# A hand-ordered decoder layer: first turn, factor additions and fifth turn rewritten

## What is computed

```python
# 1: gated recurrent attention; q = quantise a row to 8 bits, t = round a weight to -1, 0, 1
i, f, g = q(rms(x)) @ t(Wi), sigmoid(q(rms(x)) @ t(Wf)), q(rms(x)) @ t(Wg)
h[c] = f[c] * h[c - 1] + silu(i)[c] * (1 - f[c])          # scan over tokens
x = layernorm(x + q(rms(rms(g) * gw * silu(h))) @ t(Wo))
# 2: four experts, chosen by the token's id; one matrix per expert, used three times
x = layernorm(x + (silu(x @ C[e].T) * (x @ C[e].T)) @ C[e].T)
# 3: eight 512 x 512 factors
x = layernorm(x + sum_r(x @ F[r]) / sqrt(8) + bias)
```

## Time and profile before

| | us |
|---|---|
| median of 3 runs | 372.42 |
| lowest, highest | 371.88, 375.5 |
| the profiled execution, whole | 369.25 |
| its span | 367.5 |
| PE, DVE, ACT, POOL busy | 285.9, 225.3, 230.8, 200.5 |

### The profile page before, as it was taken

One profiled execution on the slowest core, in us unless ns is written; L12 is line 12 of the kernel. 1 busy time (PEld: TensorE's weight loads), 2 busy tenths in 40 slices (PEclk: granted clock), 3 DMA queues, 4 the chain that ended last, 5 costly groups with the idle time before them and its releaser, 6 DMA issues.

```text
span 367.5 us, 5728 instructions
## 1 busy us (share of the span) xinstructions
PE 285.9 (78%) x1506; PEld 215.5 (59%) x1518; DVE 225.3 (61%) x488; ACT 230.8 (63%) x456; POOL 200.5 (55%) x381
## 2 busy tenths in 40 slices
PE   1376467575687997998998895999399999999960
PEld 1254235242575675676876674777288888888640
DVE  4799999999387579839656753452234444444420
ACT  4779877977367696777777666256145555555441
POOL 2455867858546348466565837546044444444542
PEclk9998859695599999999999999899799999999996
DMA  8999968753883530003012101201401111100000
GB/s 261 389 387 374 228 117 160 143 138 89 198 162 62 94 115 2 29 40 105 0 48 75 54 29 77 69 29 42 131 29 57 52 38 59 57 30 24 28 7 0
DMA packets 17406, 37.02 MB, mean 101 GB/s; under 512 B 1503, under 2 KB 1631, under 8 KB 17376
## 3 DMA queue, kind: packets, MB, share of 16 engines
q0 software_dynamic: 6496, 15.74, 18.6%
q1 hardware_dynamic: 10880, 20.92, 17.2%
HBM read 26.68 MB, written 10.76 MB: 102 GB/s over the span
## 4 chain that ended last, share of the span: by engine, by line
PE 36%; POOL 6%; issue 6%; DMA 5%; ACT 4%; DVE 3%; POOLq 0%; ACTq 0%; DVEq 0%; SPq 0%
PE bank_m L1264 4%; PE bank_m L1268 4%; PE bank_m L1265 4%; PE bank_z L1264 3%; PE bank_z L1265 3%; DMA sorted_rows<-r,place 3%; PE bank_z L1268 3%; PE bank_y L1264 3%; PE bank_y L1265 3%; PE bank_y L1268 3%; DMA rows<-sorted_rows 2%; POOL n_d L313 2%; PE bank_tr L1235 2%; PE bank_q L1235 2%; POOL x L353 1%
## 5 line engine op out<-in xcount | busy, mean ns | idle before, releaser
L312 POOL TENSOR_SCALAR n_v<-n_dev 128x1 f32<-128x1 f32 (+1 forms) x46 | 10.1, 220 | 60.9 <-ACT x L626 28.5
L1264 PE MATMUL bank_y<-c_hi,h_hi 128*128 x76 | 32.2, 424 | 3.1 <-ACT h_hi L594 1.5
L1264 PE MATMUL bank_z<-c_hi,a_hi 128*128 x76 | 32.8, 432 | 1.9 <-ACT a_hi L594 1.9
L1264 PE MATMUL bank_m<-f_hi,m_hi 128*128 128x512 f32 x76 | 31.6, 416 | 3.4 <-DVE f_lo L876 2.6
L895 DVE TENSOR_TENSOR act_z<-bank_z,act_z 128x512 f32<-128x512 f32 x19 | 13.1, 691 | 34.3 <-ACT act_z L608 34.3
L358 POOL DMA_INDIRECT out<-r,token_of x19 | 20.6, 1087 | 23.1 <-ACT r L633 19.9
L1265 PE MATMUL bank_z<-c_lo,a_hi 128*128 x76 | 31.7, 417 | 0.0
L1265 PE MATMUL bank_y<-c_lo,h_hi 128*128 x76 | 30.8, 405 | 0.0
L313 POOL TENSOR_TENSOR n_d<-n_v,minus_half 128x1 f32<-128x1 f32 (+1 forms) x46 | 28.3, 615 | 3.8
L1265 PE MATMUL bank_m<-f_lo,m_hi 128*128 128x512 f32 x76 | 30.1, 396 | 0.0
L353 POOL TENSOR_TENSOR x<-x,bias_b 128x512 f32<-128x512 f32 x19 | 25.0, 1315 | 9.0 <-PE bank_q L1235 8.8
(11 more groups left out here) (205 smaller groups left out, 855.6 us busy)
## 6 DMA issues: line engine op xcount, KB each, us to landing
f_sum<-in_factors POOLq DMA_DIRECT2D x7, 1024.0 KB, 10.6
rows<-sorted_rows SPq DMA_DIRECT2D x19, 256.5 KB, 2.9
xs<-in_x SPq DMA_DIRECT2D x8, 512.0 KB, 6.2
c_stage<-in_ctx_t SPq DMA_DIRECT2D x4, 1024.0 KB, 14.3
sorted_rows<-pad_row SPq DMA_DIRECT2D x1, 1539.0 KB, 20.6
w_stage<-in_wf_t SPq DMA_DIRECT2D x1, 1024.0 KB, 8.4
w_stage<-in_wi_t SPq DMA_DIRECT2D x1, 1024.0 KB, 10.6
w_stage<-in_wg_t SPq DMA_DIRECT2D x1, 1024.0 KB, 12.8
```

The source lines that it names most:

```text
L1264: t.matmul(bank[:], hi[:, c, :], w_hi(c), start=(c == 0), stop=False)
```

## The change

**First turn.** SP loads factor 0 ahead of ctx(1) and x(3). POOL does `number_slots` before `weight_ready(W_F)`. DVE does `quantise_x(1)` and `order_slots` before the first weight's scale, and `rescale_f(0, 1)` only behind the rounding of W_G. PE makes the total of W_G inside `project_f(0)`, between its two halves, and ACT does `tanh_f(0, 1)` behind `weight_ready(W_G)`.

**Factor additions.** They stand at other places in POOL's list: 2 before turn 1, 3 in turn 1 behind `scale_g(1)`, 4 in turn 2 behind `power_1(0)` and ahead of `scale_o(1)`, 5 at the end of turn 2, 6 in turn 4 behind `token_of_row(1)`, 7 in turn 4 behind `scatter_rows(3)`. `high_of_factors` moves, in turn 5, from behind `silu_z(2)` to behind `forget(5, 1)`, ahead of `high_a(3)`.

**Turn 4.** It is written out apart from the loop, with another order on all engines. The loop begins with turn 5 and is otherwise the same, with the conditions on n gone.

```diff
 SP
+                sp.dma_start(f_sum[:], chunked(factors[0:D, :])).then_inc(s.factor0, 16)
                 load_ctx(1)
                 load_x(3)
-                sp.dma_start(f_sum[:], chunked(factors[0:D, :])).then_inc(s.factor0, 16)
 POOL
+                number_slots()
                 weight_ready(W_F)
-                number_slots()
...
                 power_x(2)
+                add_factor(2)
...
                         scale_g(g)
-                        add_factor(2)
+                        add_factor(3)
                         power_x(g + 2)
                     elif turn == 2:
-                        add_factor(3)
                         power_1(p - 1)
+                        add_factor(4)
                         scale_o(p)
                         pool.wait_ge(s.padded, 16)
                         scatter_rows(p - 1)
-                        add_factor(4)
                         scale_g(g)
                         power_x(g + 2)
+                        add_factor(5)
                     else:
...
-                        add_factor(5)
...
                 scatter_rows(MERGE - 1)
                 token_of_row(0)
+                g, p, n = MERGE + 1, MERGE, 1
+                scale_o(p)
+                quantise_o(p)
+                token_of_row(n)
                 add_factor(6)
+                power_2(n - 1)
+                scale_g(g)
+                number_rows(p)
+                token_of_row(n + 1)
+                power_1(p)
+                add_bias(n - 1)
+                power_2(n)
+                scatter_rows(p)
+                add_factor(7)
+                power_x(g + 2)
 ACT
                 tanh_f(0, 0)
-                tanh_f(0, 1)
                 weight_sum(W_O)
                 weight_ready(W_G)
+                tanh_f(0, 1)
...
+                square_1(p - 1)
+                high_a(n - 1)
+                square_o(p, 0)
+                norm_1(p - 1)
+                square_o(p, 1)
+                silu_z(n - 1)
+                high_h(n - 1)
...
+                square_g(g, 1)
+                high_a(n)
+                x_by_channel(g + 1)
+                max_row(g + 1)
+                square_2(n - 1)
+                silu_h(g, 0)
+                norm_2(n - 1)
+                silu_h(g, 1)
+                silu_z(n)
+                o_by_channel(p)
...
-                    if turn == MERGE + 2:
-                        high_of_factors()
...
                         forget(g, 1)
+                    if turn == MERGE + 2:
+                        high_of_factors()
                     high_a(n)
 DVE
+                quantise_x(1)
+                order_slots()
                 weight_scale(W_F)
                 round_weights(W_F)
-                order_slots()
                 weight_scale(W_I)
                 round_weights(W_I)
                 rescale_f(0, 0)
-                quantise_x(1)
-                rescale_f(0, 1)
                 weight_scale(W_G)
                 round_weights(W_G)
+                rescale_f(0, 1)
...
+                output(p, 0)
+                output(p, 1)
+                low_a(n - 1)
+                max_o(p, 0)
+                max_o(p, 1)
+                hidden(n - 1)
...
 PE
                     by_channel(g, W_F, 0, bank_c, s.zf)
+                    if g == 0:
+                        weight_total(W_G)
...
+                silu_h_by_token(p)
+                transpose_a(n - 1)
+                up(n - 1)
+                project_f(g)
+                transpose_h(n - 1)
+                project_i(g)
+                pe.wait_ge(s.o, GT * MERGE)
+                down(n - 1)
+                project_g(g)
+                transpose_a(n)
+                pe.wait_ge(s.oqt, p)
+                transpose_x(g + 1)
+                spread_max(g + 1)
+                up(n)
+                pe.wait_ge(s.xqt, g + 2)
+                transpose_o(p)
+                transpose_h(n)
+                project_back(p)
+                transpose_a(n + 1)
+                down(n)
+                pe.wait_ge(s.oqt, p + 1)
+                transpose_m(n - 1)
+                up(n + 1)
```

More of the change, by code:

```diff
@@ L448, in _ @@
                 token_of_row(0)
+                g, p, n = MERGE + 1, MERGE, 1
+                scale_o(p)
+                quantise_o(p)
+                token_of_row(n)
                 add_factor(6)
-                for turn in range(MERGE + 1, N_GROUPS + 1):
+                power_2(n - 1)
[8 more added lines that the diff above has]
+                power_x(g + 2)
+                for turn in range(MERGE + 2, N_GROUPS + 1):
                     g, p, n = turn, turn - 1, 2 * turn - LEAD
@@ L455, in _ @@
                     power_2(n - 1)
-                    if turn == MERGE + 1:
-                        add_factor(7)
                     token_of_row(n)
@@ L460, in _ @@
                         scale_g(g)
[L461 to L465, removed]
+                    add_bias(n - 2)
+                    power_3(n - 3)
+                    store(n - 3)
                     number_rows(p)
-                    if n >= 2:
-                        power_3(n - 2)
+                    power_3(n - 2)
                     token_of_row(n + 1)
                     power_1(p)
-                    if n >= 2:
-                        store(n - 2)
+                    store(n - 2)
                     add_bias(n - 1)
@@ L693, in _ @@
                         high_of_ctx(turn + 1, range(KC))
[L695 to L699, removed]
+                g, p, n = MERGE + 1, MERGE, 1
+                square_1(p - 1)
[5 more added lines that the diff above has]
+                high_h(n - 1)
+                tanh_f(g, 0)
+                tanh_f(g, 1)
+                silu_i(g, 0)
+                silu_i(g, 1)
+                forget(g, 0)
+                forget(g, 1)
+                square_g(g, 0)
+                square_g(g, 1)
[8 more added lines that the diff above has]
+                o_by_channel(p)
+                square_x(g + 2, 0)
+                high_h(n)
+                square_x(g + 2, 1)
+                high_a(n + 1)
+                square_1(p)
+                high_m(n - 1)
+                square_2(n)
+                norm_1(p)
+                norm_2(n)
+                for turn in range(MERGE + 2, N_GROUPS + 1):
                     g, p, n = turn, turn - 1, 2 * turn - LEAD
                     silu_z(n - 1)
-                    if turn == MERGE + 2:
-                        high_of_factors()
                     square_o(p, 0)
@@ L724, in _ @@
                         silu_h(g, 0)
-                    if n >= 2:
-                        high_m(n - 2)
+                    high_m(n - 2)
                     if is_group(g):
                         silu_h(g, 1)
-                    if n >= 3:
-                        square_3(n - 3)
+                    square_3(n - 3)
                     silu_z(n)
@@ L734, in _ @@
                         square_x(g + 2, 0)
-                    if n >= 3:
-                        norm_3(n - 3)
+                    norm_3(n - 3)
                     high_h(n)
-                    if n >= 2:
-                        square_3(n - 2)
+                    square_3(n - 2)
                     if is_group(g + 2):
@@ L743, in _ @@
                     square_1(p)
-                    if n >= 2:
-                        norm_3(n - 2)
+                    norm_3(n - 2)
                     high_m(n - 1)
@@ L1048, in _ @@
                     residual_1(p)
-                low_a(0)
-                for turn in range(MERGE + 1, N_GROUPS + 1):
+                g, p, n = MERGE + 1, MERGE, 1
+                output(p, 0)
[4 more added lines that the diff above has]
+                hidden(n - 1)
+                rescale_f(g, 0)
+                rescale_f(g, 1)
+                low_h(n - 1)
+                rescale_i(g, 0)
+                rescale_i(g, 1)
+                scale_x(g + 1)
+                quantise_x(g + 1)
+                gate_i(g, 0)
+                scans(g, 0)
+                gate_i(g, 1)
+                scans(g, 1)
+                residual_2(n - 1)
+                low_a(n)
+                weigh_g(g, 0)
+                weigh_g(g, 1)
+                hidden(n)
+                max_x(g + 2, 0)
+                max_x(g + 2, 1)
+                low_h(n)
+                residual_1(p)
+                low_a(n + 1)
+                residual_2(n)
+                low_m(n - 1)
+                for turn in range(MERGE + 2, N_GROUPS + 1):
                     g, p, n = turn, turn - 1, 2 * turn - LEAD
@@ L1077, in _ @@
                         scans(g, 1)
[L1078 to L1081, removed]
+                    residual_3(n - 3)
+                    low_m(n - 2)
                     if is_group(g):
@@ L1088, in _ @@
                         max_x(g + 2, 1)
-                    if n >= 2:
-                        residual_3(n - 2)
+                    residual_3(n - 2)
                     low_h(n)
@@ L1301, in _ @@
```

(16 more changed lines are left out.)

## The result

The changed kernel takes 379.78 us (median of 4 runs, 376.84 to 382.05) beside 373.57 us (median of 4 runs, 371.88 to 375.5) for the one before: ratio 1.0172, 95% interval 1.0124 to 1.0221. It is slower by 6.4 us, as forecast in size. Its profiled execution took 379.08 us, with a span of 377.3 against 367.5, so between the two profiles lie 9.8 us and not 6.4. Single executions of one kernel spread widely, those of the kernel before from 369.3 to 378.8 over the study, and its profile is the lowest of them: 369.25, where no other execution was under 369.4. The two profiles show where the loss arises; its size is taken from the ratios. The ratios leave out executions over 1.5% above the fastest of the same kernel in their job, among them three at 440.9, 716.2 and 717.3 us that nothing here explains.

The account below looks back on a forecast made before the run. It took DMA to bound up to about 50 us, DVE turns 1 to 3, PE from turn 4. Front 0, mix 5.4 and clock 1.0 gave +6.4 us on the 372.4 median: 378.8, range 372.5 to 382.5.

Parts of the forecast that it names:

- front 0: First turn and additions 2 to 5: no net effect by the end of turn 2, bounds 1.3 us gained and 3 lost.
- mix 5.4: Turn 5: the first mix starts at 148.2 instead of 142.76, 5.4 us later, and the end moves with it.
- clock 1.0: PE at the first mix: idle stretches drop its clock to half, costing 1.0 us, at most 2.5.
- Addition 7 and the first mix: Turns 4 and 5: addition 7 lands 13.5 us behind the scatter, and the mix starts 6.4 us after that.
- Turn 4: Early silu transposes and later addition 6 bring silu_z(1), and the scatter with it, 2.3 us earlier; between 1.8 and 3.2.
- rival (b): Turns 1 and 2: addition 1 lands at 46.8 as before, scale_o(0) and DVE are 3 us late, total 381.8; chance 0.13.
- The first turn's 1.3 us: First turn: DVE work moved into its idle time ahead of the first weight's scale gains about 1.3 us by turn 1.

Follow-up runs that it names:

- front_back: The changed kernel with additions 2 to 5 at their places in the kernel before: ratio to before 0.9969.
- seven_early: The changed kernel with addition 7 moved from behind scatter_rows(3) to ahead of power_1(3) in turn 4: 373.98 us, ratio to before 1.0046.
- both_back: The changed kernel with additions 2 to 5 as before and addition 7 ahead of power_1(3): ratios to before 0.9839 and 0.9897 in two jobs.
- f_lo_first_2: both_back with DVE's low_of_factors ahead of low_a(3) in turn 5, second job: ratio to before 0.9858.
- six_back: both_back with addition 6 back ahead of scale_o(3), its place before: ratio to before 0.9933.
- silu_behind_up: both_back with PE's silu transposes back behind up(0) in turn 4, and the DVE and ACT work with them: ratio to before 1.0003.
- first_turn_only: The kernel before with only the first turn's new order: ratio to before 1.0005.
- four_behind: seven_early with addition 4 behind scatter_rows(0) instead of ahead of scale_o(1): ratio to before 0.9975.
- seven_late_in_before: The kernel before with addition 7 behind scatter_rows(3) and high_of_factors behind forget(5, 1): ratio to before 1.0141.

## Why the prediction was right, and where its terms were not

**The forecast of 378.8 us is met by 379.78, but not by its terms.** It summed front 0, mix 5.4, clock 1.0. The late mix is as forecast; the front is not, and the number came out right in part by luck.

**Addition 7 and the first mix: right.** From the scatter to the first mix it had 13.5 + 6.4 = 19.9 us, measured 18.1 in two kernels and 18.3 in a third (front_back). The term that is too large is the landing: f_hi starts 12.2 us behind the scatter (145.91 - 133.70), since the addition took 11.2 us and not 12.4. The rest was 151.76 - 145.91 = 5.9 for 6.4. Slot 3's load took 6.6 us for 7.1. The late mix costs 18.1 - 11.6 = 6.5 us by the pair after and seven_early.

**Turn 4: right.** It had 2.3 us, with 1.8 "if up(0) gains no clock and 3.2 if it gains all". In after the clock did not rise (0.79 us for up(0)'s first product, as in the earlier trace rows) and the stretch is 38.3 - 36.5 = 1.8 us shorter. In both_back and f_lo_first_2 that product took 0.49 us, the full clock, and the stretch was 2.6 and 2.4 us shorter than in before. That ACT's queue takes back part of PE's gain is seen too: up(1) gains 2.2 us (19.5 for 21.7), silu_z(1) 24.1 for 25.4, which is 1.3. What the forecast treated as a sum, silu first and addition 6 later, is not one: each alone gives nothing (six_back and silu_behind_up). Against first_turn_only, where the old turn 4 took 39.9 us, the gain would be larger, so its size is known to a microsecond or so.

**The front: wrong.** "I take 0 for the front part, with bounds of 1.3 gained and 3 lost" is the step that failed. Measured by seven_early against the two both_back profiles it is 4.5 to 6.0 us lost. The mechanism was there, in the text and in rival (b), but two terms of its sum were too small. Addition 2 was given 9.0 us and up to one of contention; it took 11.8 in after, 14.3 in seven_early and 15.1 in four_behind, issued at 41.5 to 44.1 while the padding of `sorted_rows` and the load of group 4 were under way, so addition 3 landed at 66.6 and not at 61.4 to 63.4. That these two transfers made it slow was not tested. And scale_o was given 2.7 us; it took 49.93 - 45.02 = 4.9 in turn 1 and 71.38 - 67.71 = 3.7 in turn 2. The stalls came at 71.4 instead of 65.4 to 67.4. Rival (b) had named another cause, addition 1 landing at 46.8; it landed at 43.5, near the 42.8 forecast. Its effect came about all the same: DVE's quantise_o(0) is 49.96 - 47.63 = 2.3 us late in turn 1. The first turn's 1.3 us were not seen in any time.

The Trainium skill's rule of the shared ports ("SBUF — State Buffer", SBUF: two separate sides) was weighed there, and the forecast took the undisturbed 2.7 us because scale_o(0) would stand behind DVE's rounding of W_O. It did not: its first operation took 1.71 us beside DVE's second rounding, which started at 44.68. That agrees with the rule, but it does not carry the whole 4.9. In seven_early the second rounding ended at 42.68, ahead of scale_o(0), which still took 3.7 us; and in its turn 2 DVE was idle for all of scale_o(1), which took 3.1 us, its first operation 0.70 instead of 0.19. In all six places where scale_o stands right behind an addition this operation took 0.70 to 1.71 us, elsewhere up to the first mix 0.19 or 0.20, and it begins before the row of the addition's own issue (1.3 to 2.2 us) has ended. So standing behind an addition has a price of its own, which the forecast put at nothing.

**The clock: right in after, and not certain elsewhere.** PE waited 5.15 and 2.41 us ahead of the mix, the first product took 0.79 us, and the first eight cost 1.4 us more than in before. In seven_late_in_before PE had waited 5.68 and 1.46 us, and the mix ran at full clock. The forecast's bound of 2.5 us for twelve products is 2.1 by its own rows: (99.73 + 1.58 - 96.15) - (115.94 + 1.09 - 114.00).

**How it came out right in sum.** By stations, after should be 4.9 - 1.8 + 5.9 + 0.8 = 9.8 us above the profile of before, which is what the two profiles show and 3.4 more than the forecast's sum. The front's missing 4.9 us is only partly made up by a late mix that was taken too large (5.4 for 5.9 - 1.8 = 4.1). The ratio says 6.4, with 4.6 to 8.3 in its interval. The difference is the choice of profiles: that of before is 4.3 us under the median of its runs, that of after 0.7 under its own. With the front's 4.9 us in its sum the forecast would have been 383.7. Single executions of one kernel differ by up to 11.6 us (front_back), and in the two pairs of profiles of one kernel the difference arises behind the first mix. On the chain there, the scatter of group 4 alone landed in 3.4 to 4.9 us over all profiles; why was not looked into and stays open.

## What to carry to other kernels

A wait for a transfer, put into an in-order queue, is paid by everything behind it: for each addition, list what stands behind it in POOL's queue until it lands, not only what it needs, and which other engines wait for that (in four_behind the stall reached DVE through ACT). Issue a transfer where its landing time fits between the deadline of its user and the small transfers on the critical path; addition 6 had to go behind slot 1's load, addition 7 ahead of the scatter. With both, and additions 2 to 5 left where they were, the kernel was 1.0 to 1.6% faster than before, where the change as written lost 1.7%. When two edits open the same path, test each taken back alone before writing one number beside each.

## What the runs showed of the hardware

A load of 256 KB (slots 1 and 3) took 2.6 to 3.6 us with no addition beside it and 6.6 to 7.9 us when issued 2.8 to 3.7 us behind a 1 MB accumulating DMA (seven cases: 7.1 in the earlier trace rows, 7.1 in six_back, 7.9 in first_turn_only, 7.9 and 6.8 in seven_late_in_before, 6.6 in after, 6.9 in front_back). The Trainium skill ("DMA: Bandwidth & Descriptors", Queues, rings and completion order) has the engines take turns between rings, which gives an estimated 5.2 us; the measurement is longer each time. In after no packet of that queue moved from the issue of slot 3's load at 138.02 to 141.0, so most of the loss lies ahead of its first packet. The same accumulating DMA took 9.0 to 15.8 us in after, by what ran beside it. With 11.8 us for addition 2, and not the 9.0 of an undisturbed one, DVE's second stall came where it did.
